# A state-space block's sum over states: a second running sum, and three buffers of weighed blocks in place of four

## The reference, cut to what matters

```
h[t, d, n] = exp(delta[t, d] * A[d, n]) * h[t-1, d, n] + delta[t, d] * u[t, d] * B[t, n]
y[t, d]    = sum over n of h[t, d, n] * C[t, n]  +  u[t, d] * D[d]
x1 = layernorm(x + (y * silu(res)) @ W_out)
out = layernorm(x1 + (silu(x1 @ wg.T) * (x1 @ wu.T)) @ wd.T)
```

## Time and profile before

| | |
|---|---|
| median of 3 runs | 1870.64 us (1870.13 to 1873.51) |
| span of the profiled execution | 1865.8 us |
| its own time | not given beside the span; the three runs are 1870.64, 1873.51 and 1870.13 us |
| instructions | 32487 |
| mean granted TensorE clock | 0.979 of full speed |
| data read and written in HBM | 87.47 and 8.91 MB |

### The profile page before, as it was taken

The page is one execution under the profiler, slowest core; times in us unless marked ns, Lnnn a source line. Parts: engine busy times, 40 slices in busy tenths (PEclk is TensorE's granted clock), DMA queues, the critical chain, the costliest instruction groups (busy, mean ns, idle before and its releaser), DMA issues.

```text
span 1865.8 us, 32487 instructions
## 1 busy us (share of the span) xinstructions
PE 1715.3 (92%) x10128; PEld 1287.3 (69%) x10128; DVE 1705.4 (91%) x1958; ACT 1636.9 (88%) x2769; POOL 1651.8 (89%) x1629
## 2 busy tenths in 40 slices
PE   8879898998989999898998989999898998988788
PEld 3546676776767677676776767677676776767667
DVE  5989999999999999999999999999999999999994
ACT  5798988989899898998989899898998989898774
POOL 3989899998989989899898999989899898989970
PEclk9999999999999999999999999999999999999999
DMA  7213123141231314214141231313214041221100
GB/s 240 109 46 136 47 71 134 35 159 47 103 102 58 125 47 142 63 60 145 35 151 55 99 106 58 125 47 135 70 58 147 36 147 57 87 96 41 62 23 24
DMA packets 82107, 164.56 MB, mean 88 GB/s; under 512 B 10369, under 2 KB 28033, under 8 KB 81938
## 3 DMA queue, kind: packets, MB, share of 16 engines
q1 hardware_dynamic: 80498, 160.90, 25.1%
q10 hardware_dynamic: 1440, 1.58, 0.3%
HBM read 87.47 MB, written 8.91 MB: 52 GB/s over the span
## 4 chain that ended last, share of the span: by engine, by line
PE 65%; ACT 22%; POOL 7%; issue 4%; DVE 2%; DMA 0%; DVEq 0%; SPq 0%; ACTq 0%; POOLq 0%
PE fill L524 10%; PE ht_upper L699 9%; PE ht_lower L699 9%; PE y_upper L724 8%; PE fill L639 8%; POOL dbu L1185 6%; PE fill L608 5%; PE fill L629 5%; ACT da L1052 4%; ACT gt L1061 3%; PE fill L539 3%; ACT L1140 2%; ACT L1129 2%; PE fill L578 2%; ACT kb L948 2%
## 5 line engine op out<-in xcount | busy, mean ns | idle before, releaser
L1185 POOL TENSOR_TENSOR dbu<-du,brep 128x512 f32<-128x512 f32 x1024 | 1310.6, 1306 | 152.3 <-DVE h L1360 128.7
L1360 DVE TENSOR_TENSOR_SCAN h<-da,carry,dbu 128x512 f32<-128x512 f32 x960 | 1186.9, 1269 | 92.5 <-ACT da L1052 90.7
L1052 ACT ACTIVATE da<-delta,a_s 128x512 f32<-128x512 f32 x960 | 655.7, 689 | 97.2 <-DVE h L1360 89.8
L1061 ACT ACTIVATE gt<-ht_upper,ct 128x512 f32<-128x512 f32 x512 | 348.5, 681 | 62.7 <-PE ht_upper L699 55.7
L699 PE MATMUL ht_upper<-ident,h 128*128 128x128 f32 x2048 | 317.7, 278 | 67.7 <-DVE h L1360 57.3
L699 PEld LDWEIGHTS ht_upper<-ident,h 128*128 128x128 f32 x2048 | 245.9, 143 | 185.9 <-DVE h L1360 102.8
L1372 DVE SCALAR_TENSOR_TENSOR acc<-ht_lower,ct,acc 128x512 f32<-128x512 f32 x480 | 348.6, 726 | 22.4 <-PE ht_lower L699 22.4
L699 PE MATMUL ht_lower<-ident,h 128*128 128x128 f32 x2048 | 317.0, 278 | 39.4 <-DVE acc L1372 34.9
L724 PE MATMUL y_upper<-ident,gt 128*128 128x128 f32 x2048 | 316.6, 278 | 0.0
L699 PEld LDWEIGHTS ht_lower<-ident,h 128*128 128x128 f32 x2048 | 243.8, 143 | 103.0 <-issue 50.4
L724 PEld LDWEIGHTS y_upper<-ident,gt 128*128 128x128 f32 x2048 | 245.8, 143 | 72.1 <-ACT gt L1061 39.6
(11 more groups left out here) (189 smaller groups left out, 1871.9 us busy)
## 6 DMA issues: line engine op xcount, KB each, us to landing
brep<-b_rows SPq DMA_DIRECT2D x127, 512.0 KB, 3.8
xs<-xin SPq DMA_DIRECT2D x242, 256.0 KB, 2.5
xr<-x SPq DMA_DIRECT2D x16, 512.0 KB, 4.2
xt_s<-x_t SPq DMA_DIRECT2D x15, 512.0 KB, 5.1
out<-xr SPq DMA_DIRECT2D x15, 512.0 KB, 3.9
win_s<-w_in SPq DMA_DIRECT2D x2, 512.0 KB, 5.0
h<-xin SPq DMA_DIRECT2D x4, 256.0 KB, 4.0
h<-xin ACTq DMA_DIRECT2D x4, 256.0 KB, 4.5
```

The lines of the kernel that those rows point to most:

```text
L1052: nc.scalar.activation(dst[:, :], delta[:, par, m, :], ACT.Exp, scale=a_s[:, m, n:n + 1])\
L1061: nc.scalar.activation(gt[:, (n * UPPER + k) % GT, :], ht_upper[:, :], ACT.Copy, scale=ct[:, par, k, n:n + 1])\
L1185: nc.gpsimd.tensor_tensor(dbu[:, beat % DBU, :], du[:, par, m, :], brep[:, n // PIECE % 2, n % PIECE, :], ALU.mult).then_inc(dbu_ready, 1)
L1360: nc.vector.tensor_tensor_scan(h[:, n % 2, m, 0:T], da[beat % 2][:, :] if slot is None else da_ahead[:, slot, :], dbu[:, beat % DBU, :], c ...
```

## The change

The sum over states of the lower pieces is split at state SPLIT = 3. States 0 to 2 are summed in acc as before. State 3 is written by ScalarE into a new tile acc_late (one, not two), with `begin_sum` at beats 17 and 19, and VectorE adds states 4 to 15 to it. `sum_states` has nothing to do for states 0 and 3. Wherever the finished sum is turned, TensorE turns both tiles onto the same place in PSUM, which adds them. `added` and `begun` count the additions and the begun sums, for the waits. GT goes from 4 to 3, and direct_w moves from buffer 3 to the end of buffer 1.

```diff
--- before.py
+++ after.py
@@ -45,7 +45,9 @@
 
 UPPER = LOWER = 2
 TURN_AT, WEIGH_AT, ADD_AT, BACK_AT = (4, 4, 6, 7), (5, 7), (5, 7), (7, 9)
-GT = 4
+GT = 3
+
+SPLIT = 3
 
 
 READ_AT = {"conv0": 14, "conv1": 20, "conv2": 22, "conv3": 26, "ct": 48, "down0": 55, "down1": 57, "down2": 63,
@@ -117,7 +119,7 @@
     KK, DB, HB = DM // P, DI // P, HID // P
     NH = NS * DB
     NUP, NLOW = NS * UPPER, NS * LOWER
-    NSUM = (NS - 1) * LOWER
+    NSUM = (NS - 2) * LOWER
     HALF = UPPER * P
     DP = DB // 2
     PIECE = 2
@@ -182,12 +184,13 @@
         h = sb("h", [P, 2, DB, T + 1])
         carry = sb("carry", [P, NS, DB])
         acc = sb("acc", [P, 2, LOWER, DI])
+        acc_late = sb("acc_late", [P, LOWER, DI])
         gt = sb("gt", [P, GT, DI])
 
         eye = gt[:, 0, 0:GROUP]
         convw_s = gt[:, 1, 0:DB * GROUPS].rearrange("p (m g) -> p m g", m=DB)
 
-        direct_w = gt[:, 3, 0:KCONV]
+        direct_w = gt[:, 1, DI - KCONV:DI]
         direct_d = gt[:, 2, :].rearrange("p (k d) -> p k d", k=KCONV)
         kb = sb("kb", [P, HB, T])
         xr = sb("xr", [P, 2, TT, DM])
@@ -271,6 +274,18 @@
 
             if not isinstance(value, int) or value > 0:
                 eng.wait_ge(semaphore, value)
+
+        def sum_of(par, n, k):
+
+            return acc[:, par, k, :] if n < SPLIT else acc_late[:, k, :]
+
+        def added(i, n, k):
+
+            return i * NSUM + (n - 1 - (n > SPLIT)) * LOWER + k + 1
+
+        def begun(i, n, k):
+
+            return (2 * i + (n == SPLIT)) * LOWER + k + 1
 
         def fill_bank(name):
             return fill_banks[FILLS.index(name) % FILL_BANKS]
@@ -587,8 +602,9 @@
                 for k in range(2):
                     for t in range(LOWER):
                         m = 2 * pair + k
-                        mm = turn_onto(fill_bank(name)[:, k * HALF + t * P:k * HALF + (t + 1) * P],
-                                       acc[:, par, t, m * P:(m + 1) * P], k == 1 and t == LOWER - 1)
+                        for n in (0, SPLIT):
+                            mm = turn_onto(fill_bank(name)[:, k * HALF + t * P:k * HALF + (t + 1) * P],
+                                           sum_of(par, n, t)[:, m * P:(m + 1) * P], k == 1 and t == LOWER - 1 and n > 0)
                 mm.then_inc(kp_ready, 1)
 
             def turn_onto(dst, block, last):
@@ -707,11 +723,11 @@
             def turn_lower(i, n, k):
 
                 pe.wait_ge(h_ready, i * NH + (n + 1) * DB)
-                before = n * LOWER + k - 1
-                if 0 <= before < LOWER:
-                    pe.wait_ge(acc_begun, i * LOWER + before + 1)
+                j, held, nk = (i, n, k - 1) if k else (i, n - 1, LOWER - 1) if n else (i - 1, NS - 1, LOWER - 1)
+                if held in (0, SPLIT):
+                    pe.wait_ge(acc_begun, begun(j, held, nk))
                 else:
-                    after(pe, acc_done, i * NSUM + max(before - LOWER + 1, 0))
+                    after(pe, acc_done, added(j, held, nk))
                 turn(ht_lower, n, UPPER + k).then_inc(lower_turned, 1)
 
             def turn_back(i, par, n, k):
@@ -813,7 +829,8 @@
 
                 pe.wait_ge(acc_done, NCH * NSUM - (LOWER - 1 - k))
                 for m in range(DB):
-                    mm = turn_onto(tail_bank(name)[:, tile(m)], acc[:, LPAR, k, tile(m)], m == DB - 1)
+                    for n in (0, SPLIT):
+                        mm = turn_onto(tail_bank(name)[:, tile(m)], sum_of(LPAR, n, k)[:, tile(m)], m == DB - 1 and n > 0)
                 mm.then_inc(tail_filled, 1)
 
             def tail_out(name, t):
@@ -1061,10 +1078,10 @@
                 nc.scalar.activation(gt[:, (n * UPPER + k) % GT, :], ht_upper[:, :], ACT.Copy, scale=ct[:, par, k, n:n + 1])\
                     .then_inc(gt_ready, 1)
 
-            def begin_sum(i, par, k):
+            def begin_sum(i, par, n, k):
                 act.wait_ge(ct_ready, i + 1)
-                act.wait_ge(lower_turned, i * NLOW + k + 1)
-                nc.scalar.activation(acc[:, par, k, :], ht_lower[:, :], ACT.Copy, scale=ct[:, par, UPPER + k, 0:1])\
+                act.wait_ge(lower_turned, i * NLOW + n * LOWER + k + 1)
+                nc.scalar.activation(sum_of(par, n, k), ht_lower[:, :], ACT.Copy, scale=ct[:, par, UPPER + k, n:n + 1])\
                     .then_inc(acc_begun, 1)
 
             def sums(i, par, beat, first, last):
@@ -1073,8 +1090,9 @@
                     if due_now is not None and in_steps(WEIGH_AT[k], beat, first, last):
                         c, n = due_now
                         weigh(c, par if beat >= WEIGH_AT[k] else 1 - par, n, k)
-                    if beat == ADD_AT[k] and not last:
-                        begin_sum(i, par, k)
+                    for n in (0, SPLIT):
+                        if beat == ADD_AT[k] + 4 * n and not last:
+                            begin_sum(i, par, n, k)
 
             for g in range(GROUPS):
                 act.dma_start(direct_w[slice(g, P, GROUPS), :],
@@ -1362,15 +1380,15 @@
                                              carry[:, n, m:m + 1], ALU.mult, ALU.add).then_inc(h_ready, 1)
 
             def sum_states(i, par, n, k):
-                if n == 0:
+                if n in (0, SPLIT):
                     return
                 dve.wait_ge(lower_turned, i * NLOW + n * LOWER + k + 1)
-                if n == 1:
-                    dve.wait_ge(acc_begun, i * LOWER + k + 1)
+                if n - 1 in (0, SPLIT):
+                    dve.wait_ge(acc_begun, begun(i, n - 1, k))
                 else:
-                    dve.wait_ge(acc_done, i * NSUM + (n - 2) * LOWER + k + 1)
-                nc.vector.scalar_tensor_tensor(out=acc[:, par, k, :], in0=ht_lower[:, :],
-                                               scalar=ct[:, par, UPPER + k, n:n + 1], in1=acc[:, par, k, :],
+                    dve.wait_ge(acc_done, added(i, n - 1, k))
+                nc.vector.scalar_tensor_tensor(out=sum_of(par, n, k), in0=ht_lower[:, :],
+                                               scalar=ct[:, par, UPPER + k, n:n + 1], in1=sum_of(par, n, k),
                                                op0=ALU.mult, op1=ALU.add).then_inc(acc_done, 1)
 
             def sums(i, par, beat, first, last):
```

## The result

The changed kernel takes 1884.43 us (median of 4 runs, 1882.28 to 1887.13) against 1870.6 us (4 runs); the ratio is 1.007, 95% interval 1.0055 to 1.0084. The forecast was 1883.5. The profiled execution of the changed kernel has a span of 1880.5 us, 14.7 over the 1865.8 of before.

What follows compares the result with a forecast made beforehand. TensorE's queue was taken to pace the stretch holding the change, with VectorE about a microsecond ahead. Chunks 12.2 plus tail 0.7, other terms 0, gave 12.9 us: 1870.6 + 12.9 = 1883.5 us, range 1870 to 1891.

Steps and rivals of the forecast that it cites:

- TensorE, 0.87 us a chunk: Turns of the sums, beats 6 and 8: 8 more transposes at 0.109 us each come through whole, 0.87 us a chunk.
- VectorE's relief, 0: State 3's two additions leave VectorE, 1.29 us a chunk; gain taken as 0, bounds 0 and 20.6 us in all.
- The rival that VectorE was the bound: Beats 17 to 20: the freed 1.29 us a chunk come back, giving about 1852 us; chance 0.11.
- ScalarE's work, 0: Two begin_sum a chunk at beats 17 and 19, 1.16 us, covered by ScalarE's waits of 0.82 and 0.94 us; cost 0.
- a sign that the forecast is wrong: Beats 18 to 21: VectorE starting to wait for exp and TensorE for h behind it would refute the forecast.
- Moved waits, 0: Lower-block turns of states 3 and 4 wait for begin_sum, not VectorE; about 2 us to spare, cost 0.
- Three buffers, 0: Weighing j waits for turning back j-3, which TensorE's queue order already covers; cost 0, gain 0.
- 14 chunks and the tail: Chunks 1 to 14 at 0.87 us give 12.2 us; 8 more transposes before the tail's first projection give 0.7 us.
- the runs' 4.8 us over before's span: Runs' median 1870.64 us lies 4.8 us above the profiled span of 1865.8; the forecast added 12.9 to the median.

Runs made afterwards that it cites:

- e2: Kernel before, with each block of the one running sum turned twice, 8 transposes more a chunk: 1887.15 us against 1873.74, ratio 1.0071.
- e1: Changed kernel, but TensorE turns only the second running sum, so transposes are as many as before: 1872.51 us against 1873.74, ratio 0.9996.
- e5: Changed kernel with the first running sum turned twice, 8 transposes more a chunk than the changed kernel: 1899.28 us against 1873.14 for before, ratio 1.0143.
- e9: Kernel before, with one weighing a chunk (state 8, piece 0, beat 37) moved from ScalarE to VectorE: 1865.22 us against 1872.2, ratio 0.996.
- e4: Kernel before, with one more ScalarE copy at beats 17 and 19 into a spare tile, VectorE unrelieved: 1872.56 us against 1873.74, ratio 0.9999.
- e3: Kernel before, with three buffers of weighed blocks in place of four and direct_w moved: 1872.24 us against 1873.74, ratio 0.9991.
- e11: Changed kernel measured again without an edit, beside the kernel before on the same chip: 1885.58 us against 1872.2, ratio 1.0068.

## Why the prediction was right

*TensorE, 0.87 us a chunk.* Right in size, place and cause. The period grew by 0.84 us, the transposes alone give the whole loss (e2), without them it is gone (e1), and twice as many give twice the loss (e5). The choice of the queue's step over the record's 273 ns is settled by this: by the records the period would have grown by 2.2 us. TensorE's busy sum grew by 19.1 us where I forecast 14, so that sum isn't the one to judge by. The Trainium skill's figure of about 275 ns for a bf16 transpose in a kernel (TensorE: Matmul & The Clock Gate, Part 4: PE-mode transpose) agrees with the length of a float32 transpose's record here, 273 ns; it is not what one costs in this queue.

*VectorE's relief, 0.* Right. The freed time turned into waits for exp and for turned pieces. The rival that VectorE was the bound predicted 1852 us; e1, which keeps the relief and drops the price, stays at before's time. By the Trainium skill (Perfetto Trace Analysis, Optimizing Scalar/DVE Operations) a saturated VectorE may be relieved by moving work to ScalarE; that it was 91% busy didn't make it the one to relieve. In this kernel a step moved the other way, from ScalarE to VectorE, brought 7 us (e9).

*ScalarE's work, 0.* Right in the span (e4). In detail I had it wrong: exp for beats 18 and 20 came 0.5 to 0.6 us late for VectorE, where I had reckoned it in time: I compared it with VectorE's old schedule, but VectorE without its two additions comes to these scans earlier. The delay is harmless, since TensorE didn't start to wait for h: its timeline has no idle row from 850.71 to 862.97 us. I had named VectorE's waits for exp, with TensorE's for h behind them, as a sign that the forecast is wrong; the first half came true and the second didn't.

*Moved waits, 0.* Right: the turns that wait for the begun sums lie in that same stretch without an idle row.

*Three buffers, 0.* Right (e3).

*14 chunks and the tail.* 14 x 0.84 = 11.8 us came from the chunks, where 12.2 were forecast. In the tail the 16 transposes run from 1842.26 to the projection at 1844.01, 1.75 us, as reckoned (TensorE's timeline). From the last scan to the end of the span it took 45.0 us, 44.4 before: 0.6 for the forecast 0.7. From its first scan to its last the last chunk took 0.4 us less.

```profile
1842.26 0.27 PE L611 MATMUL da<-ident,acc 128*128 128x128 f32 x1
...
1844.01 1.89 PE L839 MATMUL fill<-wout_s,kb 128*128 128x256 f32 x8
```

*What makes up the rest of 14.7 us.* Three chunks of the profiled execution are 0.4 to 1.15 us longer at the second convolution of the next chunk (beats 16 and 17), where TensorE waits:

```profile
1078.74 1.06 PE L554 MATMUL fill<-xs,taps 128*32 128x512 f32 x8 [0.91 <-issue]
```

The profile names no releaser. The instruction waits for the shifted rows of xin, and the four DMA issues that load them took 4.04 us here and 2.49 us in the chunk before, so I take it for a late load; that was not tested. The trace of before has the same wait once, 0.57 us. In e11 such waits come at nearly the same times as in the changed kernel's first profile (740.37, 1080.55 and 1420.86 us for 738.60, 1078.74 and 1418.51), so they are hardly the chance of one execution; e1, which has no transpose more than before, has four of them elsewhere. Why they come stays open. Chunk 1 is 1.25 us longer, against the usual chunk, than it was before, through the clock, as told below. The sum is then 11.8 from the chunks, 0.6 from the tail less 0.4 in the last chunk, 2.4 from the three long chunks, 1.25 from chunk 1, less 0.9 for two long chunks of before: 14.75 us for the 14.7. I had added the runs' 4.8 us over before's span; the changed kernel's runs lie 1.8 us over their spans. That the forecast came within a microsecond has some luck in it. The sum had no term for late loads and for the clock in chunk 1, and the profiled execution of before seems to have been a good one, with 112.4 us for chunk 1; its own time isn't on record, so that these differences cancel is an inference.

## What to carry to other kernels

When two engines look full, look at which results lie ready: here h lay ready 0.9 us before TensorE took it, so VectorE's work could be cut for nothing, while each step on TensorE's queue cost its full length. Price an instruction of a full queue by the distance of starts, not by the length of its record. The same 0.57 us of ScalarE were free at beats 17 and 19 and worth 0.57 us at beat 37: before work is moved between engines, find the stretch where the relieved engine is waited for, and check who waits for the engine that takes it.

## What the runs showed of the hardware

TensorE's granted clock falls to 1.2 GHz in or behind stretches in which TensorE waits, and that is not the same in each execution. Windows of the kernel before (first line) and of e1 and e4 (second and third), from 140 to 150 us, where chunk 1 begins behind a stretch that GpSimd paces:

```profile
140.00:150.00 10.00, 8.29 (x38) 4.97 (x39) 8.69 (x9) 6.71 (x12) 9.92 (x10) 1.00 0.34 129
```

```profile
140.00:150.00 10.00, 7.86 (x32) 5.22 (x33) 9.02 (x9) 5.91 (x10) 9.92 (x10) 0.83 0.22 71
```

```profile
140.00:150.00 10.00, 7.82 (x29) 4.92 (x30) 8.13 (x9) 5.38 (x9) 9.92 (x10) 0.66 0.16 52
```

The clock columns are 1.00, 0.83 and 0.66. The same instructions in the three timelines of TensorE, from a turn to the turning back behind four projections:

```profile
142.78 0.63 PE L699 MATMUL ht_upper<-ident,h 128*128 128x128 f32 x4 [1.41 <-DVE h L1360]
...
145.50 0.60 PE L724 MATMUL y_upper<-ident,gt 128*128 128x128 f32 x4
```

```profile
143.20 1.00 PE L715 MATMUL ht_upper<-ident,h 128*128 128x128 f32 x4 [1.41 <-DVE h L1378]
...
147.50 0.60 PE L740 MATMUL y_upper<-ident,gt 128*128 128x128 f32 x4
```

```profile
143.25 1.08 PE L701 MATMUL ht_upper<-ident,h 128*128 128x128 f32 x4 [1.41 <-DVE h L1367]
...
148.40 0.68 PE L726 MATMUL y_upper<-ident,gt 128*128 128x128 f32 x4
```

From 144 to 146 us the granted clock is 1.00 in the first and 0.50 in the other two, which is 1.2 GHz. The pieces take 2.72, 4.30 and 5.15 us, without an idle row between: 1.58 and 2.43 us more at the lower clock. Chunk 1 takes 112.41 us (first scan to first scan) in the profiled execution of before, and 114.05 and 114.94 in the two others, 1.64 and 2.53 more, while their usual chunks are as long as before's. In the changed kernel this piece takes 3.99 us (142.80 to 146.79). So the clock accounts for nearly all of chunk 1's difference. Why it fell in these executions and not in that of before stays open: the waits ahead are the same in all three, 1.29 and then 1.41 us. I had not expected this. A comparison of two single executions would have seen this as a part of the change; the chunk period doesn't.
